# Butterfly stages as matrices grown on the chip, packed loads, later raw masks and a merged gate and linear pass

## The reference

```python
# layer 0, unit: expand, butterfly, gelu, butterfly, contract
for stage in range(10):                 # dim = 1024, s = 2 ** stage
    yr = y.reshape(*lead, nb, 2, s); a, b = yr[..., 0, :], yr[..., 1, :]
    na  = w[..., 0, 0] * a + w[..., 0, 1] * b
    nb2 = w[..., 1, 0] * a + w[..., 1, 1] * b
    y = jnp.stack([na, nb2], axis=-2).reshape(*lead, dim)
...
# layer 1, unit: linear plus low-rank experts, top 2 of 8 by a softmax gate
x @ W_lin.T + sum_e weight_e * (x @ left_e) @ right_e
...
# layer 2, unit: ternary weights
wq = clip(round(w / mean(abs(w))), -1, 1) * mean(abs(w))
```

## Time and profile before

| | us |
|---|---|
| median of three runs | 2759.05 |
| the three runs | 2755.01, 2760.55, 2759.05 |
| profiled execution | 2750.75 |
| its span, first to last instruction | 2749.0 |
| PE busy | 2553.4 (93%) |
| DVE busy | 1709.7 (62%) |
| ACT busy | 1085.9 (40%) |
| POOL busy | 935.2 (34%) |
| mean granted TensorE clock | 0.989 |

### The profile page before, as it was taken

The page is one execution under the profiler, slowest core; times in us unless marked ns, Lnnn a source line. Parts: engine busy times, 40 slices in busy tenths (PEclk is TensorE's granted clock), DMA queues, the critical chain, the costliest instruction groups (busy, mean ns, idle before and its releaser), DMA issues.

```text
span 2749.0 us, 54741 instructions
## 1 busy us (share of the span) xinstructions
PE 2553.4 (93%) x21625; PEld 1716.8 (62%) x21625; DVE 1709.7 (62%) x4702; ACT 1085.9 (40%) x1811; POOL 935.2 (34%) x2408
## 2 busy tenths in 40 slices
PE   5989988899999998899999998889999999889999
PEld 3447654477776754467776765447777675446776
DVE  6863678955543478984544368985554347887442
ACT  4744445522224444542323354552222443454221
POOL 1023233244432233234443233324443323324333
PEclk9999999999999999999999999999999999999999
DMA  4020000000000000000000000000000000000000
GB/s 177 1 91 11 2 11 14 2 1 9 9 9 13 8 12 2 13 2 8 9 9 9 11 12 2 11 1 7 6 8 8 17 1 12 1 2 1 5 5 8
DMA packets 18733, 36.99 MB, mean 13 GB/s; under 512 B 3600, under 2 KB 13872, under 8 KB 17456
## 3 DMA queue, kind: packets, MB, share of 16 engines
q1 hardware_dynamic: 18480, 33.48, 3.5%
HBM read 29.28 MB, written 4.19 MB: 12 GB/s over the span
## 4 chain that ended last, share of the span: by engine, by line
PE 69%; DVE 18%; ACT 5%; issue 4%; POOL 3%; SPq 1%; DMA 0%; DVEq 0%; ACTq 0%; POOLq 0%
PE P L1260 8%; PE P L1119 5%; PE P L1144 4%; PE P L1293 4%; PE P L1278 4%; PE P L1131 4%; PE P L1261 4%; PE P L973 4%; PE P L1072 4%; PE P L1080 4%; PE P L1269 4%; PE P L1052 4%; DVE mx L1677 3%; ACT ET L1433 3%; PE P L849 2%
## 5 line engine op out<-in xcount | busy, mean ns | idle before, releaser
L1677 DVE TENSOR_REDUCE mx<-P 128x8 f32<-128x1232 f32 x256 | 367.6, 1436 | 191.9 <-PE P L978 108.7
L1260 PE MATMUL P<-xT,w 128*128 128x256 f32 x1024 | 264.0, 380 | 1.1 <-DVE R L1897 0.5
L1728 DVE SCALAR_TENSOR_TENSOR x<-P,w_gates,x 128x512 f32<-128x512 f32 x112 | 83.7, 747 | 259.0 <-PE P L1294 114.1
L1433 ACT ACTIVATE ET<-P 128x2048 f32<-128x2048 f32 x96 | 180.2, 1877 | 161.0 <-PE P L1055 93.8
L1260 PEld LDWEIGHTS P<-xT,w 128*128 128x128 f32 x1024 | 192.4, 190 | 66.5 <-issue 29.8
L745 POOL TENSOR_TENSOR sm<-sm 128x2 f32<-128x2 f32 x384 | 75.4, 196 | 464.3 <-DVE sm L1673 444.2
L973 PE MATMUL P<-KB,R 32*128 32x308 f32 x1536 | 163.6, 477 | 48.6 <-ACT ET L1433 27.3
L1386 ACT ACTIVATE xn<-x,sm 128x256 f32<-128x256 f32 x256 | 139.1, 592 | 164.4 <-POOL sm L753 164.4
L1890 DVE SCALAR_TENSOR_TENSOR gu<-gu,P 128x256 f32<-128x256 f32 x128 | 53.7, 420 | 237.4 <-ACT gu L1484 237.4
L1484 ACT ACTIVATE gu<-P 128x256 f32<-128x256 f32 x128 | 49.0, 382 | 323.1 <-PE P L1261 298.4
L1052 PE MATMUL P<-R,KB 32*128 32x256 f32 x2048 | 161.7, 402 | 1.7 <-DVE mx L1677 1.2
(11 more groups left out here) (307 smaller groups left out, 5715.5 us busy)
## 6 DMA issues: line engine op xcount, KB each, us to landing
kvw<-in_wkv SPq DMA_DIRECT2D x12, 672.0 KB, 4.1
x<-in_x SPq DMA_DIRECT2D x16, 256.0 KB, 2.7
out<-x SPq DMA_DIRECT2D x16, 256.0 KB, 2.1
w<-in_w SPq DMA_DIRECT2D x2, 1024.0 KB, 8.8
w<-in_wexp SPq DMA_DIRECT2D x1, 1028.0 KB, 7.4
w_w<-in_wcon SPq DMA_DIRECT2D x1, 1024.0 KB, 9.4
R<-in_m3t SPq DMA_DIRECT2D x1, 1024.0 KB, 10.5
R<-in_w1q SPq DMA_DIRECT2D x1, 1024.0 KB, 12.3
```

The costliest lines, as they stand in the source:

```text
L1260: e.matmul(o, wm[:, c, js], s.xT[:, c, :], start=n == c == 0, stop=False, skip_group_check=True)
L1433: e.activation(ET[:].rearrange("p g c -> p (g c)"), quad.rearrange("p g c -> p (g c)"), ACT.Exp, bias=mb1[:, b:b + 1] if l == 1 else 0.0). ...
L1677: e.tensor_reduce(s.mx[:, i, :, 2 * u:2 * u + 2], quad[:, :, 0:2 * NK].rearrange("p g (a k) -> p g a k", a=2), AX.X, ALU.max).then_inc(q_d, 1)
```

## The change

- Near stages: instead of 112 multiplications of a group with a stage matrix, the product of the seven stage matrices of a group is grown on the chip. `grow` has seven steps a side. A step multiplies the matrix so far with two selection matrices (`pick`) on PE and takes the product with the weights of the stage (`wt`) on DVE; it serves all eight groups at once, and the matrix doubles in width each time. Then `near` multiplies each group once. The result of side 1 goes straight to `wdn`, so `down_there` goes.
- Loads: sixteen small constants become one (`first`), the butterfly tables one (`tab`), `gl` joins `lin`. The order is new. The bias scaling moves from the head of DVE's queue to a planned step `gb`. The load of `wkv1` no longer waits for the masks.
- Raw masks and raw layer 2 weights are loaded in `raw` when the folding is done, into places that it used. `masks`, `tsum` and `tern` run behind the first attentions of streams 2 and 3. The three passes of `tern` move from DVE to POOL.
- Unit of layer 1: `gate1` multiplies with all 296 columns of linear, gate and low-rank weights, into two banks that stay held; `lin_` only adds the low-rank part to them, and DVE adds the two halves to x in two instructions.
- Planner: costs of the new steps, earliest times of loads (`lands`), new offsets, and 130 and 34 in place of 10 and 3 for how far a stream is and for its number.

```diff
@@ sets of loads
-        FIRST = ("gates", "fmq", "fmqb", "sgn", "fmv", "fmvb", "negc", "selc", "tm")
-        MID = ("bd2", "rev", "wq1", "wo1", "bq", "bk", "lin", "gl", "right", "wo2", "nw", "g3", "a1", "a3")
-        LATE = ("wq2", "b1q", "wq3", "wo3", "w1", "w3", "w2", "b1", "b3", "a2", "b2")
+        FIRST = ("first",)
+        MID = ("wq1", "wo1", "lin", "right", "wo2", "a1", "a3")
+        LATE = ("wq2", "b1q", "wq3", "wo3")
+        LAST = ("w1", "w3", "w2", "b1", "b3", "a2", "b2")
@@ turns
-            if s.i == 3:
-                yield ("masks",)
...
+            if s.i >= 2:
+                k = s.i - 2
+                for t in range(7):
+                    yield "grow", k, t
+                yield "done", ("grown", k)
+                if k:
+                    for i in range(3):
+                        yield "wide", 1, i
+                    yield "after", "near"
+                else:
+                    yield "after", ("grown", 1)
...
+                    yield "near", k, j
...
+                    yield ("raw",)
...
+                    if b == 0 and s.i == l + 2:
...
+                        yield "after", "raw"
+                        if l == 0:
+                            yield ("masks",)
+                            yield "done", "masks"
+                        yield "tsum", l
+                        yield "tern", l
...
@@ orders
-                i, p = min(can, key=lambda c: (start(c[1]) + BACK[c[1][2]].get(c[1][1], 0) + 10.0 * count[c[0]] + 3.0 * c[0],
+                i, p = min(can, key=lambda c: (start(c[1]) + BACK[c[1][2]].get(c[1][1], 0) + 130.0 * count[c[0]] + 34.0 * c[0],
@@ sp_program
-            for s in S[:2]:
-                load_x(s, 0)
-            for n in FIRST:
-                load(n, l_first)
+            load("first", l_first)
+            e.dma_start(tabs[:, 0:320], d["tab"]).then_inc(l_tab, 16)
+            load_x(S[0], 0)
             load_ctx(0)
+            e.dma_start(pick, d["pick"]).then_inc(l_tab, 16)
+            e.dma_start(xu[0], d["wexp"]).then_inc(l_xu, 16)
+            load_x(S[1], 0)
+            e.dma_start(xd[0], d["wcon"]).then_inc(l_xd, 16)
...
+            def raw():
 
                 e.wait_ge(d_up, 1)
-                e.wait_ge(a_dn, 1)
...
+                e.wait_ge(a_near[1], 4)
+                e.wait_ge(d_near[1], 4)
+                e.dma_start(m1r, d["m1"].partition_broadcast(128)).then_inc(l_mask, 16)
...
@@ pool_program
+            def tern(c):
+
+                raw, to = ((w1r, w1i), (w2r, w2i))[c]
+                e.wait_ge(d_quant, c + 1)
+                e.tensor_scalar(raw, raw, wsc[:, 4 + c:5 + c], MAGIC, ALU.mult, ALU.add).then_inc(g_tern, 1)
...
@@ pe_program
+            def grow(k, t):
...
+                n, st_ = (16, 32, 64, 128, 256, 256, 256)[t], min(t, 5)
+                for x in range(2):
+                    t_ = e.matmul(P[:, 6 + k, 256 * x:256 * x + n], pick[:, 5 - st_ if k == 0 else 1 + st_, x, :], of, start=True,
+                                  stop=True)
+                t_.then_inc(p_grow[k], 1)
...
+                e.matmul(o, near_m[k][:, j, :], xu[0][:, j, :] if k == 0 else xd[1][:, j, :], start=True,
                          stop=True).then_inc(p_near[k], 1)
...
-            def gate1(s, k):
-                o = take(k)
+            def gate1(s, k0, k1):
+
+                o = [take(k) for k in sorted((k0, k1))]
                 e.wait_ge(s.a_t, s.t)
                 for i in range(2):
                     for c in range(2):
-                        t = e.matmul(o[:, 40 * i:40 * i + 40], s.xT[:, c, 128 * i:128 * i + 128], gl[:, c, :],
-                                     start=c == 0, stop=c == 1)
+                        t = e.matmul(o[i][:, 0:296], s.xT[:, c, 128 * i:128 * i + 128], lin[:, c, :],
+                                     start=c == 0, stop=False, skip_group_check=True)
...
-                for i in range(2):
-                    o = bank[:, 256 * i:256 * i + 256]
-                    for c in range(2):
-                        e.matmul(o, s.xT[:, c, 128 * i:128 * i + 128], lin[:, c, :], start=c == 0, stop=False)
-                    t = e.matmul(o, s.tlT[:, 128 * i:128 * i + 128], right[:, :], start=False, stop=True)
+                for i, k in enumerate(sorted((k0, k1))):
+                    t = e.matmul(P[:, k, 0:256], s.tlT[:, 128 * i:128 * i + 128], right[:, :], start=False, stop=True,
+                                 skip_group_check=True)
@@ dve_program
+            def grow(k, t):
+                e.wait_ge(p_grow[k], t + 1)
...
+                    e.tensor_tensor(to.rearrange("p (j c x) -> p j c x", j=J, x=2), by.rearrange("p x (j c) -> p j c x", j=J),
+                                    w.unsqueeze(2).broadcast_to([128, J, n // J, 2]), ALU.mult).then_inc(d_grow[k], 1)
...
```

More of the change, by code:

```diff
@@ L4 @@
 from contextlib import ExitStack
[L6 to L9, removed]
+import itertools
+NIN = ["x", "ctx", "m1", "m1t", "m3", "m3t", "first", "fcw", "wexp", "wcon", "tab", "pick",
+       "bias", "dnb", "wq1", "wq2", "wq3", "wkv1", "wkv2", "wkv3", "wo1", "wo2", "wo3",
+       "lin", "right", "w1q", "b1q", "w2q", "w1", "w3", "w2", "a1", "a3", "b1", "b3", "a2", "b2"]
 class Tally:
@@ L335, in late, with lands @@
             return []
+        def lands(name, of, engine):
+            if name == "norm" and engine == "DVE" and of[1] == of[2] == 0:
+                return (6000.0, 9500.0, 16500.0, 17000.0)[of[0].i]
+            if engine == "PE" and name in ("key", "val") and of[0] == of[1] == 0:
+                return 6500.0
+            if engine == "PE" and name in ("grow", "near"):
+                return 7500.0 if name == "grow" else 10500.0
+            return 14000.0 if name == "wide" and of[0] == 1 else 16000.0 if name == "gb" else 0.0
         def half(name, j):
@@ L343, in early @@
                 return "back", of[1]
-            if (name, engine) in (("mat", "DVE"), ("near", "PE")):
+            if name == "near" and engine != "PE":
                 return name, *of
@@ L446, in turns @@
                     yield "bias", s, b, 4 + l
+                    if b == 0 and l == 2:
+                        yield "after", ("tern", 0)
+                        yield "after", ("tern", 1)
+                    if b == 0 and l == 3:
+                        yield "after", "late"
                     if l != 2:
@@ L575, in start @@
             def start(p):
-                return max(when(p[4] + also(p)), free[p[2]], *(let[w][n][0] for n, w in enumerate(takes(p[1], p[6], p[2]))))
+                return max(lands(p[1], p[6], p[2]), when(p[4] + also(p)), free[p[2]], *(let[w][n][0] for n, w in enumerate(takes(p[1], p[6], p[2]))))
             while True:
@@ L605, in orders @@
                     bank[at_] = got
-                folded = {("upt", "DVE", 6): 6, ("near", "ACT", 55): 7}.get((p[1], p[2], of[-1])) if of else None
+                folded = {("upt", "DVE", 6): 6, ("near", "ACT", 7): 7}.get((p[1], p[2], of[-1])) if of else None
                 back = list(bank.get(at_, ()))
@@ L686, in store @@
                     load_x(s, b + 1)
-            stages = {"masks": masks, "late": late, "kvw": kvw_next, "store": store}
+            stages = {"raw": raw, "late": late, "kvw": kvw_next, "store": store}
             for name, *of in ORDER["SP"]:
@@ L1296, in f3 @@
                 free[k] = [(s.d_x, X.up(s.d_x))]
-            stages = {"fill": fill, "near": near, "upt": upt, "tsum": tsum, "down_there": down_there, "key": key, "val": val,
+            stages = {"fill": fill, "grow": grow, "near": near, "upt": upt, "tsum": tsum, "key": key, "val": val,
                       "turn": turn, "qp": qp, "sc": sc, "mt": mt, "st": st, "sts": sts, "s2": s2, "pv": pv, "pz": pz, "out": out_,
@@ L1916, in f3 @@
                 residual(s, gates[:, 7:8], k, False)
-            stages = {"masks": masks, "mat": mat, "near": near, "wide": wide, "upt": upt, "tsum": tsum, "tern": tern,
+            stages = {"masks": masks, "gb": gb_, "grow": grow, "near": near, "wide": wide, "upt": upt, "tsum": tsum, "tern": tern,
                       "val": val, "norm": norm, "mx": mx, "split": split, "no": no, "out": out_, "down": down,
```

482 lines of the change are left out of this document (242 added, 240 removed), and 4 rows, old and new, of the table BACK.

## The result

The changed kernel takes 2716.39 us (median of 4 runs, 2712.70 to 2717.71), the kernel before in the same session 2758.74 us. The ratio is 0.9846 (95% interval 0.9829 to 0.9863): 42 us less, where 81 were forecast. Its profiled execution has a span of 2714.5 us, against 2749.0: 34.5 us less, not 42, because the profiled execution before lay 8 us under its median. Tables made from the two profiles therefore end at 34.5.

The account below looks back on a forecast made before the run. PE (TensorE), busy 93%, was taken as the bound, with 120.8 us of prologue cost in reach. Prologue -77, POOL +5, linear unit -4, planner -5 gave -81 us: 2678, with 2645 to 2718 holding 8 in 10.

Parts of the forecast that it names:

- Prologue, -77: First 200 us: new folding, 24 us on PE, cuts a prologue cost of 120.8 to 44; bounds -52 and -94.
- Passes on POOL, +5: Six quantization passes moved from DVE to POOL delay steps in POOL's queue; 5 us lost, bounds 0 and 20.
- rival A: POOL's passes (lock, in-order queue) and the wait for the masks stop other engines, 15 us each: 2708; chance 15%.
- Linear unit, -4: Layer 1 unit: merging saves 14 us of PE, 8 gained, 4 lost to held banks; bounds -18 and +30.
- Rival C: Linear unit: two held banks make PE wait, kernel slower than before; 2770 at 6 us a visit; chance 5%.
- Planner, -5: New order of the whole run: priced at nothing, bounds 20 us either way, less 5 for streams closer together.
- Rival D: Whole run: new order uses the slack, 8 us less per batch, linear unit's gain at upper bound: 2645; chance 14%.
- Rival B: Prologue: growing is as slow as the old stages, folding ends near 100 us: 2720; chance 8%.
- if passes on POOL exceed 6 us: Sign for the quantization passes: the prediction is wrong if they take over 6 us on POOL.
- 640 to 650 us apart: Sign for the repeated batches after the prologue: they again follow each other at 640 to 650 us.
- Wrong if PE is idle over 35 us before 125 us: Sign for the early part of the run: more than 35 us of PE idle before 125 us refutes the prediction.
- sign of held banks: Linear unit: the prediction is wrong if PE waits appear behind a held bank while a gate is open.

Follow-up runs that it names:

- e1: Changed kernel with the three quantization passes per weight back on DVE, same order: 2703.69 us, ratio 0.9810.
- e8: Changed kernel with passes on DVE and e2's filler, all planner offsets searched anew: 2699.68 us, ratio 0.9797.
- e9: As e8, but with the linear unit split as before the change, no bank held, offsets searched anew for it: 2737.91 us, ratio 0.9926.
- e3: Changed kernel in its own order, both banks still held, the 256 linear columns multiplied again in the second step: 2743.01 us, ratio 0.9950.
- e2: Changed kernel with filler from 400 ns of expected idle instead of 900, 0.9 of the gap instead of 0.6: 2704.16 us, ratio 0.9816.
- e10: Kernel before the change with e2's filler rule, nothing else: 2747.79 us, ratio 0.9960.
- e11: Changed kernel with passes on DVE and filler from 250 ns of expected idle, all of the gap: 2687.48 us, ratio 0.9746.

## Why the prediction came out half right

- **Prologue, -77: right.** Key (0, 1) is 71.5 us earlier, inside the bounds of 52 to 94. First matmul 6.62 (6.5 forecast); growing 14.9 and `near` 11.4 on PE, 26.3 together (24). One part was off and cost nothing: the folding ended at 80 us, not 55, since the second `near` waits for `wide` on ACT and DVE and runs from 49.5 to 61. The raw masks are issued at 80.2 us and DVE no longer stands at them; key (0, 1) came at 160 all the same, so their cover held.
- **Passes on POOL, +5: mis-sized.** They take 14.5 us a weight, 29 in all (bounds 12 to 35, 30 taken). What the term counted was POOL's queue; what cost most was DVE's stand, 15.9 us less the 7.5 that left DVE, and the end lost 10 to 13, inside the bounds of 0 to 20. This is the lock of rival A without its wait for the masks; A's 2708 lies near 2716, but half of its loss, the masks' 15 us, did not come. What did not hold was "PE has four streams to draw on". At the first weight PE did 988 instructions from 150 to 270 us where e1 did 1032, and 5.7 us were gone by key (0, 2). The second weight falls where DVE is the fuller engine, as the window of 250 to 500 us of the changed kernel has it:

```profile
250.00:500.00 250.00, 204.64 (x2023) 117.89 (x2016) 215.77 (x595) 117.38 (x158) 91.61 (x257) 0.92 0.07 27
```

- **Linear unit, -4: mis-sized, twice.** The merging saves 26.6, not 14: the rows alone give 17.4, and that about half of it falls where DVE is the fuller engine has nothing for it, as the saving came through whole and more. No run shows the 4 us for held banks: e8 against e9 has the merged unit 36 us ahead with its banks held. Rival C, which had them turn the whole change into a loss, did not occur.
- **Planner, -5: the step that failed.** From before to e3, which has the new prologue and order and the old unit's work, the lead of 73.7 us at key (0, 1) (231.8 against 158.1) shrinks to 7.2 at the end (2749.0 against 2741.8). Of these 66.5 us POOL's passes explain 10 to 13, so some 54 went with the order, 14 a batch; the bounds were 20 for the whole run either way. That is the order with all that hangs on it: where the clock is full it costs 3 to 6 us a batch, and behind key (0, 1) the clock falls more often, which by the estimate above is worth 10 to 25 us in the changed kernel. How the rest divides is open. The changed kernel gets 27 back by the merging. "The order can't be priced from rows" was true, but a new order of every queue was then priced near nothing, although showed that the old one repeats to within ten instructions and leaves PE 37 us of idle a batch. The sum, roughly: -72 (prologue) + 13 (POOL) - 27 (unit) + the order's part makes -42 only if the order's part is +44, clock included (54 by e3), where -5 was forecast. The time that came, 2716.39, lies within the 2645 to 2718 that the prediction gave 8 in 10, but barely, and not by its mechanism: the unit gained 23 us more than its term, which hid part of what the order lost. With the unit as forecast this sum puts the kernel near 2739.
- **Rival D** had the new order use the slack; it was the reverse. Rival B gave 2720, the nearest figure of all, by a growing as slow as the old stages; that did not occur: the growing ran from 8.6 to 23 us.
- **Signs named in advance.** Wrong "if passes on POOL exceed 6 us": they did (7.11). Batches "640 to 650 us apart": 651 to 656. Both pointed the right way. "Wrong if PE is idle over 35 us before 125 us" did not trigger (25). Nor did the sign of held banks: no wait of PE in the changed kernel's trace ends at L1853, DVE's sum that frees them.

What stays open: which property makes the old order better than two found by the planner's estimate, and why the clock falls more often in the new ones. Between key (2) and key (3) of a batch e9 takes 131 us and before 123; the rest lies between key (3) and the next key (1), 427 against 421 (430 in the changed kernel). The merged unit in the old order was not tried, nor a third order at a full clock.

## What to carry to other kernels

Price an instruction that moves to POOL by what DVE may be doing beside it, since a long pass can stop DVE's shortest instruction for its whole length; here 16 us of standing on DVE, against 7.5 us of work taken off it, made the end 10 to 13 us later. When a change brings a new order of everything, the order is a term of its own with bounds as wide as the gain; undo the work and keep the order (as e3 does) to read it, and compare stretches with the same granted clock, or the clock's price is booked on the order. An edit that gains as much on both kernels has not cleared a cause until the cause is gone in both (e2 left 58 us at the lower clock where e10 left none). A large wait in a list is not spare time until an experiment moves it.

## What the runs showed of the hardware

- A `tensor_scalar` over 128x2048 on POOL took 1.98, 7.11 or 5.37 us by its operation (scale and add; add and min; max to bf16), where DVE took 1.29, 1.23 and 1.23.
- Beside these passes a DVE `tensor_scalar` over two columns stood for 6.9 us, while batch-norm, reciprocal and transpose instructions did not stand. What tells them apart was not tested.
- 143 memsets of one column on POOL held a DVE pass from its start to their end, 3.9 us, though each is recorded at 0.1 us: this train of short instructions left DVE no gap.
- Filler raised the mean clock from 0.975 to 0.987 (e2) and to 0.992 (e11, with the passes on DVE) and paid after the prologue. In the prologue it raised the clock of a quarter from 0.66 to 0.93 and paid nothing.
- Two groups of matmuls made one saved more than their rows show: 1.66 us a visit against 1.09, with a spread of 0.5. Why was not tested.
